# First norm on ScalarE, first weights loaded at once, and the first layer by column chunks

## The reference

```python
xn = _layernorm(x, axis=-1)                       # (x - mean) / sqrt(var + 1e-5), per row
x1 = relu(xn @ W_ah + b_ah)                       # the first layer
xs = [relu(gat_conv(x1, src, dst, W, a_s, a_d, b)) for W, a_s, a_d, b in three_layers]
x = x + relu(concat(xs) @ W_out + b_out) + mix(xn)   # mix: attention by random features, from xn
x = experts(_layernorm(x))
```

## Time and profile before

| | us |
|---|---|
| median of three runs | 1809.81 |
| the profiled execution, device time | 1810.71 |
| its span in the trace | 1809.0 |
| PE busy | 1595.9 (88%) |
| DVE busy | 1179.4 (65%) |
| first matmul of the first layer starts | 47.05 |
| first matmul of the three layers `h` starts | 131.52 |
| first load of a filled table starts | 562.64 |

### The profile page before, as it was taken

How to read it: one execution, slowest core, us unless ns; L and a number is a source line. 1 busy time by engine, 2 the same in 40 slices (tenths; PEclk the granted TensorE clock), 3 DMA queues, 4 the chain that set the end, 5 groups by cost and what they waited for, 6 DMA issues and landing times.

```text
span 1809.0 us, 24889 instructions
## 1 busy us (share of the span) xinstructions
PE 1595.9 (88%) x9701; PEld 1208.5 (67%) x9701; DVE 1179.4 (65%) x2532; ACT 647.5 (36%) x1257; POOL 538.8 (30%) x311
## 2 busy tenths in 40 slices
PE   3799999999997787999899699969999998764987
PEld 2456666556665665888888688868889875544665
DVE  7677553114444697897988999969769735656233
ACT  2331111122224766766665333334434412331110
POOL 1387687767750000111221211222212110001331
PEclk9899999999998998999999899989999999885999
DMA  7424434354424226213213443354133114534951
GB/s 219 128 41 116 105 79 116 61 99 89 95 53 162 85 78 191 83 33 113 92 32 109 141 155 111 130 163 144 38 98 127 63 56 165 201 129 147 332 153 59
DMA packets 196904, 207.43 MB, mean 115 GB/s; under 512 B 83759, under 2 KB 153533, under 8 KB 196786
## 3 DMA queue, kind: packets, MB, share of 16 engines
q1 hardware_dynamic: 118514, 186.24, 31.3%
q0 software_dynamic: 78272, 19.59, 7.9%
HBM read 141.62 MB, written 65.27 MB: 114 GB/s over the span
## 4 chain that ended last, share of the span: by engine, by line
PE 71%; DVE 16%; DMA 4%; ACT 3%; issue 3%; SPq 1%; POOL 0%; POOLq 0%; DVEq 0%; ACTq 0%
PE bank L971 17%; PE bank L816 13%; PE bank L818 13%; PE bank L817 13%; PE bank L1137 3%; PE bank L1125 3%; DVE eb L1407 3%; PE bank L996 2%; DVE eb L1416 2%; PE bank L1024 2%; DVE junk L1370 2%; DMA mi<-mixed_rows 2%; PE bank L918 1%; DVE q_max L1439 1%; ACT ef L1815 1%
## 5 line engine op out<-in xcount | busy, mean ns | idle before, releaser
L971 PE MATMUL bank<-hb,eb 128*128 128x193 f32 (+3 forms) x2400 | 429.3, 337 | 38.7 <-DVE eb L1416 33.8
L971 PEld LDWEIGHTS bank<-hb,eb 128*128 128x128 f32 (+3 forms) x2400 | 409.6, 194 | 51.2 <-DVE eb L1416 38.0
L1966 POOL DMA_INDIRECT table<-amount,place x170 | 341.8, 2011 | 162.9 <-DMA table<-amount,place 74.8
L1977 POOL TENSOR_TENSOR node<-node,rinv 128x960 f32<-128x960 f32 (+2 forms) x36 | 62.6, 1751 | 813.0 <-DVE rinv L1429 813.0
L1407 DVE SCALAR_TENSOR_TENSOR eb<-shift_b,as_low,shift_b 128x640 f32<-128x640 f32 (+1 forms) x240 | 231.6, 1006 | 7.0 <-DMA shift_b<-shift_rows 7.0
L1785 ACT ACTIVATE eb<-eb,asd 128x640 f32<-128x640 f32 (+1 forms) x240 | 182.6, 815 | 138.6 <-DVE eb L1407 138.6
L1416 DVE SCALAR_TENSOR_TENSOR eb<-eb,count 128x1280 f32<-128x1280 f32 (+1 forms) x120 | 200.4, 1670 | 0.0
L1370 DVE CUSTOM_DVE_ANT_0 junk<-ab,absent 128x1250 bf16<-128x1250 f32 x120 | 175.0, 1458 | 1.3
L816 PE MATMUL bank<-w_o_hi,aT_hi 128*128 128x384 bf16 (+1 forms) x360 | 120.6, 335 | 0.4 <-DVE won L1585 0.4
L817 PE MATMUL bank<-w_o_lo,aT_hi 128*128 128x384 bf16 (+1 forms) x360 | 120.4, 334 | 0.0
L818 PE MATMUL bank<-w_o_hi,aT_lo 128*128 128x384 bf16 (+1 forms) x360 | 120.2, 334 | 0.0
(11 more groups left out here) (280 smaller groups left out, 2918.8 us busy)
## 6 DMA issues: line engine op xcount, KB each, us to landing
w<-in_w SPq DMA_DIRECT2D x16, 1152.0 KB, 17.9
shift_b<-shift_rows SPq DMA_DIRECT2D x24, 625.0 KB, 6.3
h_rows<-h_row SPq DMA_DIRECT2D x27, 388.0 KB
hb<-h_rows SPq DMA_DIRECT2D x12, 873.0 KB
ar<-node_rows SPq DMA_DIRECT2D x27, 384.0 KB
qk_rows<-qk_row SPq DMA_DIRECT2D x12, 625.0 KB
ab<-as_rows SPq DMA_DIRECT2D x12, 625.0 KB, 5.7
stage<-in_W SPq DMA_DIRECT2D x18, 384.0 KB
```

Of the source, the lines that this page charges most:

```text
L971: ins = T.matmul(bank[w // 2][0:M, c0:c0 + GC + 1], p[0:K, u, w * P:w * P + M], hv[0:K, t, 0:GC + 1], start=opens and u == 0 and w % 2 == ...
L1966: G.indirect_dma_start(tables[i], bass.IndirectOffsetOnAxis(place[:, c:c + 1], axis=0), amount16[:, c:c + 1], None, compute_op=ALU.add).th ...
```

## The change

- The norm moves from VectorE to ScalarE, as an activation with a scale and a bias for each row; VectorE gets one small operation more per batch (bias = -mean times the scale). There are four batches of tiles now, (0, 1), (2, 3, 4), (5, 6, 7), (8, 9), and statistics of later tiles stand between turned tiles.
- All six blocks of `W_ah` are loaded at the start, from ScalarE's queue, into `stage` and three new buffers `w_first`. Their low parts are computed on POOL.
- The first layer goes by chunks of columns: `x1` step n is chunk n // 6 and feature block n % 6, so it needs only the first four tiles (first chunk) or eight (second). It starts after tile 3; tiles 4 to 9 are turned one by one between its first six products. The steps of the keys follow after the tiles, and `w_part` n // 3 now stands behind products 2, 5, 8, ...
- The tables are filled with zeros from SP's queue, right after the loads of x and of the edges, and ahead of `a_row` and `stage<-in_W`. The transfers themselves have the same shape.

```diff
 def first_nodes():
-    for m in range(KD):
-        if m == 0:
+    for n in range(KD * NC):
+        if n == 0:
             yield "a_in", 0
-        yield "w_part", m
-        for c in range(NC):
-            yield "x1", NC * m + c
-            yield None
+        yield "x1", n
+        if n % NC == NC - 1:
+            yield "w_part", n // NC
+        yield None
...
+def first_tiles():
+    yield from (("ln_tile", 0), ("ln_tile", 1), ("ln_root", 0), ("ln_tile", 2))
+    stats = {0: (("ln_tile", 3), ("ln_tile", 4), ("ln_root", 1)), 1: (("ln_tile", 5),), 2: (("ln_tile", 6),),
+             3: (("ln_tile", 7), ("ln_root", 2)), 4: (("ln_tile", 8),), 5: (("ln_tile", 9), ("ln_root", 3))}
     for t in range(NT + 1):
         if t < NT:
             yield "norm", t
         if t:
             yield "turn", t - 1
+        for j in {0: (0, 1), 1: (2, 3), 2: (4, 5)}.get(t, ()):
+            yield "w_split", j
+        yield from stats.get(t, ())
+        yield None
     yield "keys", 0
     yield "h_set", 0
...
             def x1(n):
-                m, c = divmod(n, NC)
+                c, m = divmod(n, KD)
...
-                pe.wait_ge("turned_lo", 2 * NT)
+                pe.wait_ge("turned_lo", 2 * -(-c1 // P))
...
+            def w_first_(_):
+                for j in range(KD):
+                    A.dma_start(w_views(j)[0], w_from(j)).then_inc(sem[w_count(j)[0]], 16)
...
+            def norm(t):
+                R = rows(t)
+                se.wait_ge("ln_stat", norm_count(batch_of(t) + 1))
+                se.wait_ge("turned", 2 * (t - 1))
+                A.activation(xn[t % 2][0:R, :], x_tile(t)[0:R, :], ACT.Identity, bias=stats[0:R, t, 12:13],
+                             scale=stats[0:R, t, 14:15]).then_inc(sem["xn_ready"], 1)
...
+            def w_split(j):
+                if j < KD:
+                    buf, parts = w_views(j)
+                    ge.wait_ge("w_hi", j + 1)
+                    G.tensor_tensor(parts[1], buf, parts[0], ALU.subtract).then_inc(sem["w_lo"], 1)
...
             def edges_in(_):
                 for i, d in enumerate((src_cols, dst_cols)):
                     S.dma_start(cols[i][:, :], d).then_inc(sem["edge_cols_in"], 16)
+                sy.wait_ge("set_up", 1)
+                for b, (t0, t1) in enumerate(BATCHES):
+                    sy.wait_ge(f"x_in{b}", 16 * (t1 - t0))
+                none = zero[:, :].bitcast(U16)
+                for table in tables:
+                    S.dma_start(table[0:N * N, :].rearrange("(p t n) o -> p t (n o)", p=EP, n=N),
+                                none[0:EP, 0:N].unsqueeze(1).broadcast_to([EP, N // EP, N])
+                                ).then_inc(sem["table_zero"], 16)
+                    S.dma_start(table[N * N:, :], none[0:EP, 0:1]).then_inc(sem["table_zero"], 16)
```

More of the change, by code:

```diff
@@ L51 @@
 NC = len(COLS)
-BATCH = NT // 2
+BATCHES = ((0, 2), (2, 5), (5, 8), (8, 10))
+NEAR = 4
 HALF = NT // 2
@@ L80, in alike, with norm_count, batch_of, w_count @@
     return ([(t0, t0 + len(full), P)] if full else []) + [(t, t + 1, rows(t)) for t in range(t0 + len(full), t1)]
+def norm_count(b):
+    return sum(2 * (t1 - t0) + 7 for t0, t1 in BATCHES[:b])
+def batch_of(t):
+    return next(b for b, (t0, t1) in enumerate(BATCHES) if t0 <= t < t1)
+def w_count(j):
+    return (f"w_in{j}", 16) if j < KD else (f"w_in{j % 3}", 16 * (j // 3))
 def halves_of(d):
@@ L161, in first_order @@
             yield "norm", t
-        if t == 0:
-            yield "ln_stats", 1
         if t:
             yield "turn", t - 1
[L166 to L170, removed]
+        for j in {0: (0, 1), 1: (2, 3), 2: (4, 5)}.get(t, ()):
+            yield "w_split", j
+        yield from stats.get(t, ())
+        yield None
     yield "keys", 0
     yield "h_set", 0
-    yield from paced((first_nodes(), 1), (key_steps(), 1))
+def first_order():
+    yield "x_in", 0
+    yield "w_first", 0
+    yield "edges_in", 0
+    tiles = first_tiles()
+    for _ in range(NEAR + 1):
+        for step in tiles:
+            if step is None:
+                break
+            yield step
+    yield from paced((first_nodes(), 1), (itertools.chain(tiles, key_steps()), 1))
 def projection_steps(done):
@@ L559, in program @@
         r_a = cursor[0] = after_count
-        xs = put("xs", [P, NT, D])
+        xs = [put("xs0", [P, NEAR, D])]
+        cursor[0] = r_a + size([P, NT, D], F32)
         r_b = cursor[0]
@@ L681, in program @@
         cursor[0] = r_e
+        w_first = [put(f"w_first{i}", [128, D]) for i in range(3)]
+        assert cursor[0] <= r_f
+        cursor[0] = r_e
         hb = [put("hb0", [P, NT, HW]), hb1]
@@ L704, in program @@
         assert cursor[0] <= 229368
+        cursor[0] = r_f
+        xs.append(put("xs1", [P, NT - NEAR, D]))
+        r_bias = cursor[0]
         cursor[0] = r_f
@@ L734, in by_tiles, with x_tile @@
             return d[t0 * P:t1 * P, :].rearrange("(t p) c -> p t c", p=P), d[FULL * P:N, :]
+        def x_tile(t):
+            return xs[0][:, t, :] if t < NEAR else xs[1][:, t - NEAR, :]
         def w_from(j):
@@ L753, in w_views @@
             if j < 6:
-                return buf[:, 0:D], [w[:, j, 0:D] for w in wg[0]]
+                return (buf if j < 3 else w_first[j - 3])[:, 0:D], [w[:, j, 0:D] for w in wg[0]]
             if j < 24:
@@ L1155, in vector_program @@
             V.memset(ones[:, :], 1.0).then_inc(sem["set_up"], 1)
-            for rest in (asd, diag, m_col, shift):
+            for rest in (asd, diag, m_col):
                 V.memset(rest[:], 0.0)
@@ L1166, in keys, with ln_tile, ln_root @@
                 V.tensor_copy(spare[:, :], spare_i[:, :]).then_inc(sem["keys"], 1)
-            def ln_stats(b):
-                ve.wait_ge("set_up", 3)
[L1170 to L1181, removed]
+            def ln_tile(t):
+                R = rows(t)
+                b = batch_of(t)
+                st = stats[0:R, t, :]
+                n = norm_count(b) + 2 * (t - BATCHES[b][0])
+                ve.wait_ge("set_up", 3)
+                ve.wait_ge(f"x_in{b}", 16 * (BATCHES[b][1] - BATCHES[b][0]))
+                V.bn_stats(st[:, 0:6], x_tile(t)[0:R, 0:D // 2])
+                V.bn_stats(st[:, 6:12], x_tile(t)[0:R, D // 2:D]).then_inc(sem["ln_stat"], 1)
+                ve.wait_ge("ln_stat", n + 1)
+                V.bn_aggr(st[:, 12:14], st[:, 0:12]).then_inc(sem["ln_stat"], 1)
+            def ln_root(b):
+                bs = slice(*BATCHES[b])
+                mean, v, r, u = (stats[:, bs, i] for i in (12, 13, 14, 15))
+                n = norm_count(b) + 2 * (bs.stop - bs.start)
                 ve.wait_ge("ln_stat", n)
@@ L1193, in ln_stats @@
                 V.tensor_tensor(r, r, u, ALU.mult).then_inc(sem["ln_stat"], 1)
[L1195 to L1200, removed]
+                ve.wait_ge("ln_stat", n + 6)
+                V.scalar_tensor_tensor(mean, mean, -1.0, r, ALU.mult, ALU.mult).then_inc(sem["ln_stat"], 1)
             def turn(t):
@@ L1217, in h_set @@
             def h_set(_):
+                ve.wait_ge("w_lo", KD)
+                V.memset(shift[:, :, :], 0.0)
                 for b in h_out:
@@ L1916, in hidden @@
                                  bias=b1c[:, e, f:f + 1]).then_inc(sem["gelu"], 1)
-            mine = dict(keys=keys, ln_stats=ln_stats, turn=turn, w_split=w_split, w_part=w_part, x1=x1, h=h,
+            mine = dict(keys=keys, w_first=w_first_, ln_root=ln_root, norm=norm, turn=turn, w_split=w_split,
+                        w_part=w_part, x1=x1, h=h,
                         feats_in=feats_in, v=v, qk_split=qk_split, count=count_, edge_exp=edge_exp, evict=evict, k_exp=k_exp,
@@ L1942, in edges_in @@
             def edges_in(_):
[L1943 to L1951, removed]
                 G.memset(halves[:, :], 1.0).then_inc(sem["pool_set"], 1)
```

38 lines of the change are left out of this document (18 added, 20 removed), and 6 rows, old and new, of the table TAKEN_OVER.

## The result

The changed kernel takes 1874.82 us (median of 4 runs, 1870.89 to 1880.09), the kernel before 1811.88 beside it (1808.46 to 1814.71): a ratio of 1.035, 95% interval 1.031 to 1.039. It is slower, as forecast, but by 63 us and not by 11.5.

A forecast was written before the change was run, and what follows sets the result against it. PE is full from 131.5 to 563 us, so the start of the layers `h` moves everything after it. Later PE resumption 14.7 - 7.8 + 0.9 + 2.9 + 0.8 = +11.5 on 1809.8 gives 1821.3 us; range 1805 to 1840.

The forecast's parts named there:

- Start-up: Norms on ScalarE, low parts on POOL: first product at about 32 us, not counting because PE stops later anyway.
- The zeros on SP's queue: The deciding term: 6.25 MB on five engines at 123.5 GB/s, 50.6 us, ending at 72.1.
- Rival B: Zeros use 6.5 engines as on POOL's queue, ending at 60.4: -0.6 us, 1809; chance 0.06.
- The landing of `stage`: Loads queued behind the zeros on SP's queue, wanted by the first `w_part`, land at 75.6 us.
- From the landing to PE: Sums, high part, norm of tile 7 and its halves take 5.0 us; PE resumes at 80.7.
- From PE's resumption to the end of `h`: Stretch after PE's stop: -7.8 products already done, +0.9 key transposes, +2.9 tile turns, +0.8 waits.
- waits 0.8: PE's waits in the last six short products, with `w_part` 5 behind the last: 5.9 us against 5.1, 0.8 more.
- After that: PE full until 563, so all stays; indirect transfers start at about 104, last at 555; slack 19 us instead of 38.
- Rival A: Later loads on SP's queue are not held up by the zeros, PE's stop goes: -19.8 us, 1790; chance 0.15.

The follow-up runs named there:

- t1: Changed kernel with each table's last 125 entries zeroed as one 250-byte piece from one partition, still on SP's queue: 1849.8 us, ratio 1.020.
- t11: Kernel before, with each table's last 125 entries zeroed as one 250-byte piece from one partition, on POOL's queue: 1814.1 us, ratio 0.999.
- t8: t4 with the six `w_part`s each ahead of a wide product and one key step per two narrow products: 1801.7 us, ratio 0.995.
- t12: t10 with one key step for each narrow product again, `w_part`s still ahead of wide products: 1801.6 us, ratio 0.995.
- t2: Changed kernel with tables rounded up, each zeroed by one transfer from 128 partitions without tail, still on SP's queue: 1821.3 us, ratio 1.004.
- t4: Changed kernel with the zeros, same shape and tails, issued on POOL's queue behind its sixth low part: 1819.1 us, ratio 1.003.
- t10: t8 with the tables also zeroed by transfers from 128 partitions, on sixteen engines: 1801.6 us, ratio 0.993.

## Why the prediction was wrong

- *Start-up*: better than forecast. First product 29.30 (32); POOL's low parts 1.64 and 1.61 us each (4.84 for three), below the bounds of 1.98 to 2.71 from the earlier trace rows; ScalarE's norm 1.01 to 1.03 (0.84). None of it counts, as foreseen, since PE stops later.
- *The zeros on SP's queue*: the engines and their rate were right. Issued at 19.15 (19.4), 29.8% of 16 engines, 111 to 121 GB/s (123.5). The Trainium skill's rule ("DMA: Bandwidth & Descriptors", section "Why a DMA increments its semaphore by 16 and not by 1") agrees with it: 5 of 16 is 31%. Rival B's 6.5 engines of the earlier trace rows did not show on this queue. **What failed is that the tails got no term**: two transfers of 250 bytes each, priced at nothing. They cost 26.6 us of the stop (t1), nearly all of the 28.1 by which PE's resumption was off. With one-piece tails it came at 82.17, 1.5 us from the forecast. The row to see it was there: behind its zeros the kernel before moved 0.55 MB from 21 to 31 us, 55 GB/s, and 1.72 MB without the 2-byte pieces (t11). The landing of `stage` is 103.5, not 75.6. The same page of the Trainium skill says, in "Specifications", that below 512 B an engine reads, modifies and writes. The runs here show some 13 us for each 125 pieces of 2 bytes (half of the 26.6); whether reading and modifying is the reason, no run shows.
- *From the landing to PE*: 5.0 forecast, 103.55 to 108.78, 5.2. Right.
- *From PE's resumption to the end of `h`*: the other failure, the term "waits 0.8". Forecast 254.4 - 3.2 = 251.2 us from PE's resumption to `as_row` (before: 320.4 - 65.97); it is 383.2 - 108.78 = 274.4, 23 more. I noted that the six narrow products stand in a row and that VectorE has more to do there, and then carried over the size of the old waits. I named `w_part` 5 there, but two more (3 and 4, behind products 11 and 14) meet the narrow products. PE's idle time in this stretch is 20.8 us, against 5.9 before and 6.7 by the forecast: 14 more. PE is busy for 253.6 us, against 248.6 before and 244.6 by the forecast: 9 more, with the clock at 0.50 behind two of the stops (from 165.9 to 168.6 and from 180.0 to 184.3 us). That makes the 23. t8 takes 22.3 us off `as_row`; 4.9 of them are key steps that only move (t12), the rest is the place of `w_part`.
- The two together are 28 + 23 = 51 us, and 11.5 + 51 = 63, which is the measured difference.
- *After that*: right in that PE stays full; the tables are read at 626.5 (562.6 + 63.9). The last indirect transfer starts at 587.7, 38.8 us earlier, so the slack did not shrink as I had put it (to 19); the first, forecast at 104, starts at 141.3, and the two losses delayed both ends alike.
- *Rival A* (no stop, 1790) was tested by t2 and t4: a stop of 4.6 and 2.7 us only, and yet 1821 and 1819. Its -19.8 left out the second loss as well. With both losses out, t8 and t10 reach 1801.6, not 1790.

What stays open: why 125 pieces of 2 bytes make the large pieces behind them slow (on POOL's queue they do it too, see t11, only nothing waited for it there); why SP stands at the issue; and a part of the 11 us to rival A's sum. Of these 11 us, 6.6 lie between `as_row` and the first load of a table (248.8 us in t10, 242.2 before), where key steps now stand that were done ahead of `as_row` before; the rest was not looked for.

## What to carry to other kernels

Before a transfer is moved to another queue, list everything that stands behind it there and ask when the queue will take the next issue; a small transfer behind a long one is not free, and 125 pieces of 2 bytes cost as much as 1.6 MB of the zeros (an estimate: 13 us at 120 GB/s). Shape fills so that they use all engines (here 128 partitions instead of 125), or put them behind the loads that someone waits for. When a loop is reordered, look for where its short steps end up: work that was hidden by a long step every third time must be placed again, beside the long ones.

## What the runs showed that was not expected

- Behind 125 pieces of 2 bytes from 125 partitions SP's queue moved 13 GB/s for 16 us, at the busy share of five engines (120 GB/s with one piece of 250 bytes, t1). The pieces themselves are recorded at 9 ns each; the 2500-byte pieces behind them took up to 8.1 us instead of 0.11.
- SP stood at the issue of a small transfer for 17.4 and 23.9 us behind a long one of 125 partitions (t1), and for 6.3 us at the first load behind two long ones of 128 partitions, which were themselves issued in 1.35 us (t2). POOL in the kernel before began the first of its four at 15.38, and was at its next operation at 20.14.
- POOL subtracts 128x768 bf16 from f32 into bf16 in 1.6 us, less than its f32 operations of the same size.
